# Slot layer of a transformer decoder: the statistics of a later pair's x are issued ahead of the candidate's input on VectorE

## The reference

```python
x = x + slot_layer(_layernorm(x, axis=-1))

def _layernorm(x, axis=-1, eps=1e-05):
    m = jnp.mean(x, axis=axis, keepdims=True)
    v = jnp.var(x, axis=axis, keepdims=True)
    return (x - m) / jnp.sqrt(v + eps)

def slot_layer(x):                         # per sequence, 64 slots
    h = gelu(ctx @ w1.T + b1)              # ctx: x beside the mean of the slots
    route_logits = (h @ w2.T + b2) / (abs(tau) + 0.1)
    topk_vals, topk_idx = top_k(route_logits, 8)
    alpha = softmax(topk_vals) scattered to the 64 slots
    gi = (alpha.T @ x) / (alpha.sum(axis=1) + 1e-08)
    r = sigmoid(xr + hr)                   # a GRU cell: gx = gi @ w_ih.T + b_ih, gh = S @ w_hh.T + b_hh
    z = sigmoid(xz + hz)
    n = tanh(xn + r * hn)                  # the candidate
    h_new = (1.0 - z) * n + z * hs
    return alpha @ (h_new @ wv.T + bv) @ wo.T + bo
```

## Time and profile before

| | us |
|---|---|
| median of 3 runs | 1517.61 |
| the runs | 1512.31, 1517.61, 1517.75 |
| time of the profiled execution | 1513.51 |
| its span, first to last instruction | 1511.8 |
| slot layer's statistics and steps, from the first f_stats to the end | 1218.0 to 1511.8 |
| f_stats of the slot layer, 64 instructions | 0.41 each |

### The profile page before, as it was taken

One profiled execution on the slowest core, in us unless ns is written; L12 is line 12 of the kernel. 1 busy time (PEld: TensorE's weight loads), 2 busy tenths in 40 slices (PEclk: granted clock), 3 DMA queues, 4 the chain that ended last, 5 costly groups with the idle time before them and its releaser, 6 DMA issues. The chain is left out here.

```text
span 1511.8 us, 57218 instructions
## 1 busy us (share of the span) xinstructions
PE 1416.7 (94%) x22238; PEld 1064.8 (70%) x22238; DVE 1101.2 (73%) x3030; ACT 888.3 (59%) x1541; POOL 873.5 (58%) x1184
## 2 busy tenths in 40 slices
PE   6999999999999999985999999999999859999997
PEld 4777777777777777764777777777777636666664
DVE  6777777777777777653667676767676658989896
ACT  3555555555555555542666666666667347777773
POOL 3455555555555555542577777777777635555543
PEclk9999999999999999998999999999999969999998
DMA  5400000000000000003000000000000000010101
GB/s 165 135 2 1 0 0 0 0 0 0 0 0 0 0 0 0 2 3 120 17 24 14 21 14 21 14 21 14 21 14 8 2 1 29 29 35 28 35 28 42
DMA packets 31207, 32.40 MB, mean 21 GB/s; under 512 B 3937, under 2 KB 29602, under 8 KB 31138
## 3 DMA queue, kind: packets, MB, share of 16 engines
q1 hardware_dynamic: 31138, 31.46, 6.9%
HBM read 23.06 MB, written 8.39 MB: 21 GB/s over the span
## 5 line engine op out<-in xcount | busy, mean ns | idle before, releaser
L1028 POOL TENSOR_SCALAR_AFFINE_SELECT a_probs_t<-a_probs_t 128x512 f32<-128x512 f32 x256 | 161.9, 666 | 77.8 <-ACT a_probs_t L697 77.8
L1560 DVE TENSOR_REDUCE c_neg_max<-score_banks 128x8 f32<-128x512 f32 (+1 forms) x128 | 116.3, 950 | 80.2 <-PE score_banks L1292 80.2
L1042 POOL TENSOR_TENSOR a_less<-a_attn,a_remote 128x512 f32<-128x512 f32 x32 | 40.8, 1275 | 218.0 <-DVE a_attn L873 218.0
L1713 POOL TENSOR_SCALAR_AFFINE_SELECT c_probs_t<-c_probs_t 128x512 f32<-128x512 f32 x256 | 154.7, 639 | 12.3 <-ACT c_probs_t L1487 12.1
L1487 ACT ACTIVATE c_probs_t<-score_banks 128x2048 f32<-128x2048 f32 x64 | 120.2, 1879 | 27.2 <-PE score_banks L1320 27.2
L384 PE MATMUL side_banks<-a_xn_t,a_w_qk 128*128 128x256 f32 x512 | 134.4, 398 | 1.7 <-ACT a_xn_t L642 0.7
L697 ACT ACTIVATE a_probs_t<-score_banks 128x2048 f32<-128x2048 f32 x64 | 120.2, 1878 | 25.9 <-PE score_banks L541 25.9
L850 DVE TENSOR_REDUCE a_neg_max<-score_banks 128x8 f32<-128x512 f32 (+1 forms) x128 | 116.4, 951 | 6.0 <-PE score_banks L511 6.0
L384 PEld LDWEIGHTS side_banks<-a_xn_t,a_w_qk 128*128 128x128 f32 x512 | 93.0, 196 | 13.1 <-issue 2.4
L2141 POOL TENSOR_TENSOR r_hn<-rz_t,half_hn 128x256 f32<-128x256 f32 x32 | 23.4, 730 | 123.4 <-ACT rz_t L1970 123.4
L652 ACT ACTIVATE a_k_z<-side_banks,a_b_k,row_half 128x256 f32<-128x256 f32 x128 | 61.8, 562 | 54.0 <-PE side_banks L384 54.0
(11 more groups left out here) (263 smaller groups left out, 3927.7 us busy)
## 6 DMA issues: line engine op xcount, KB each, us to landing
x_sb<-in_x SPq DMA_DIRECT2D x32, 256.0 KB, 2.9
c_ctx_in<-in_ctx SPq DMA_DIRECT2D x32, 256.0 KB, 2.7
out<-y SPq DMA_DIRECT2D x32, 256.0 KB, 2.1
w_ih<-in_ffn_w_ih SPq DMA_DIRECT2D x1, 768.0 KB, 6.4
w_hh<-in_ffn_w_hh SPq DMA_DIRECT2D x1, 768.0 KB, 7.1
a_raw_qk<-in_attn_qk_w SPq DMA_DIRECT2D x1, 512.0 KB, 4.3
a_raw_cross<-in_xattn_qk_w SPq DMA_DIRECT2D x1, 512.0 KB, 4.7
b_ih<-in_ffn_b_ih SPq DMA_DIRECT2D x1, 384.0 KB, 6.1
```

The source lines that it names most:

```text
L1028: nc.gpsimd.affine_select(out=probs, in_=probs, pattern=[[0, 4], [1, 128]], compare_op=ALU.is_ge, fill=0.0, base=-1, channel_multiplier=-1 ...
L1560: ins = nc.vector.tensor_reduce(neg_max[:, tt, :].rearrange("p (i s l) -> p i s l", i=4, s=2)[:, :, :, late], all_scores[:, :, :, 128 * (1 ...
L1713: nc.gpsimd.affine_select(out=heads, in_=heads, pattern=[[0, 4], [1, 128]], compare_op=ALU.is_ge, fill=0.0, base=0, channel_multiplier=-1) ...
```

## The change

In VectorE's `step`, the call of `candidate(updated)` moves from ahead of `norm_stats(second)` to behind it. The wait for the routing logits and the wait for the moments stand ahead of `norm_stats` as before, and so ahead of the candidate now. No instruction is added, removed or resized; the order of the other engines is the same.

```diff
                 if norms:
                     norm_moments()
-                if updated.real:
-                    candidate(updated)
                 if routed.real:
                     dve.wait_ge(logit_ready, routed.count(1, 1))
                 if at.real and second.real:
                     dve.wait_ge(ln_step, following.count(2, 2))
                     norm_stats(second)
+                if updated.real:
+                    candidate(updated)
                 if routed.real:
                     route_top(routed)
                     route_mark(routed)
```

## The result

The changed kernel takes 1521.51 us (median of 8 runs, 1516.55 to 1524.26); the kernel before took 1514.11 us beside it (8 runs, 1512.15 to 1517.75). The ratio is 1.0038 with a 95% interval of 1.0023 to 1.0053: 5.8 us slower, within 0.5%. The two medians lie 7.4 us apart and the means of the runs 5.9 us; the ratio goes with the means. The profiled execution took 1516.55 us.

A forecast was written before the change was run, and what follows sets the result against it. A ring through n_in, h_n, f_x_bias and f_xn was taken as the bound, not VectorE. Terms 0.9 + 1.95 - 0.5 = +2.3 us on 1513.5 gave 1515.8; forecast 1517.8, between that and 1519.9, range 1511.5 to 1524.

The forecast's parts named there:

- The ring: Slot step: chain from rz through n_in, h_n, f_x_bias, both f_xn and back to rz sets its 8.32 us.
- Step one: Ahead of n_in: f_stats waits 0.15 us behind f_moments, so n_in is 0.31 us late in the loop.
- third rival: At n_in: hardly late, 0.08 us in the loop, f_xn stays held; +1 us, 1514.5; 0.13 with mixtures within 0.5%.
- Step two: At f_x_bias: first f_xn slips in ahead, second waits; 0.25 us gained against 0.31 lost, net +0.06 a step.
- first rival: At f_x_bias: f_xn loses its turn in every step; +6.1 us, 1519.6; chance 0.33.
- The sum: Whole layer: inner steps +0.9, first and written-out steps +1.95, step 3 -0.5, total +2.3 us.
- the inner steps' term: Loop: 15 inner steps at +0.06 us each, +0.9 us.
- The two groups of times: Kernel before: its four times fall into 1512.3 and 1513.5, 1517.6 and 1517.8; a median after may lie in either.
- second rival: VectorE's list: it is the bound and the gap is filled; 11 us less, 1502.2; chance 0.09.

The follow-up runs named there:

- late_only: Changed kernel with the pair of f_stats done a second time behind n_in, into a spare tile: 1518.62 us, ratio 1.0047 to the kernel before.
- turn: Changed kernel with slot_val placed between the two f_xn, so the first is issued while h_n works: 1513.51 us, ratio 0.9979 to the kernel before.
- wait_hn: Changed kernel with one more wait on POOL, f_x_bias waiting until h_n is written: 1520.09 us, ratio 1.0052 to the kernel before.
- split: Changed kernel with one f_stats left ahead of n_in and the other put behind it: 1516.79 us, ratio 0.9999 to the kernel before.
- park_split: Changed kernel with one f_stats on each side of n_in and f_x_bias at the head of POOL's step, double-buffered: 1506.26 us, ratio 0.9934.

## Why the prediction was right and where it was wrong

**The bound was right.** The ring over n_in, h_n, f_x_bias and the end of f_xn fits every run in which f_x_bias stands behind h_n: late_only added 0.66 us of VectorE work for nothing, and only the three kernels with f_x_bias parked went clearly below 8.3 us a step. One partner was overlooked: in the kernel before neg_top lasts 0.33 us in place of 0.17, held by h_n, so work taken from behind n_in meets a first stop there and a second at f_x_bias.

**Step one was right.** f_stats starts 0.14 us behind the second f_moments in the loop (taken: 0.15); n_in is 0.30 late in inner steps (0.31), 0.14 in a round's first (0.14), 0.25 in written-out steps (0.25). The chain of waits of the changed kernel shows the register work ahead of f_stats (start, length):

```profile
1308.29 0.06 DVEq L1992
1308.35 0.05 issue
1308.40 0.10 DVE f_stats L1992
```

The Trainium skill's rule that a semaphore between VectorE instructions costs nothing extra ("VectorE: DVE Perf Modes", "The DRAIN you can't avoid") would have put f_stats ahead of f_moments' end, as neighbours without a wait stand. It came 0.14 us behind it in the loop, and 0.10 (rz + 2.58 against 2.48) where there is no register work. The trace disagrees with the rule for this pair, and the third rival falls with it.

**Step two failed**, where it said "I take it that the first f_xn slips in between h_n and f_x_bias". The places were forecast well: slot_val at rz + 4.55 both in forecast and trace, f_xn issued 0.05 us ahead of f_x_bias (forecast 0.06). In the other inner steps the lead was 0.02 or 0.03. But f_xn lost its turn in every inner step, lasting 1.43 to 1.47 us. I took the recorded starts for the order of asking, on the strength of one row of another shape in another layer. The rows of the c_xn pair, which I also leaned on, don't show a thin lead: there the first c_xn starts 0.43 us ahead of POOL's c_summed (767.99 against 768.42), as far as in turn. Leads of 0.02 to 0.07 us lose, leads of 0.17, 0.34 and 0.45 win. The argument that the prediction gave the first rival, that part of an f_xn's 0.40 us passes before it touches what POOL holds, is the one that fits; the f_xn of wait_hn that runs through its first 0.09 us beside h_n unheld bears it out. Why a_gate got through with 0.02 us was not tried. The Trainium skill's rule ("SBUF — State Buffer", "Who interferes with whom") says that whoever issues first holds the lock for a whole instruction. The second half agrees with every row here; the first half holds only if issue isn't read as the start that the profile records.

**The sum.** With the turn lost, each of the inner steps costs nearly n_in's whole delay (0.28 of 0.30 us), not 0.06. Turn gave 0.25 us of it back, by the order on VectorE alone and with n_in as late. The first rival's sum was +6.1 us; measured +5.8, of which +5.6 stand in the slot steps. Its terms measured: 15 inner steps 4.3 (4.65), first steps of rounds 0.6 (0.7), written-out steps 1.1 (1.25; step 28 has a delay of 0.18 and lost 0.15), step 3 -0.56 (-0.5), and +0.2 in the last three steps, where n_in was 0.06 to 0.08 late, which no term had. The forecast's own sum was +2.3, so the inner steps' term, +0.9 where 4.3 was measured, is the one that failed. The time, 1521.5 us, lies in the range on its upper side, and that is no merit of the forecast: the top of the range was taken from the first rival and from the spread of the runs. The two groups of times that stood behind the 1517.8 were an accident of four runs: in the 19 runs taken later the kernel before fills the space between them, from 1512.56 to 1519.16 us.

**The second rival** (VectorE bound, 11 us gained) is refuted for this kernel by the loss itself and by late_only. In the kernel with f_x_bias parked the same edit gains 12.7 us, about what this rival had promised; whether VectorE's list is the bound there was not shown.

## What to carry to other kernels

A gap on a busy engine is worth filling only if no later instruction swallows what is won: compare each instruction's length in the step with its shortest (f_xn 0.72 against 0.40, neg_top 0.33 against 0.17), since a wait for the other engine hides in the length and counts as busy. Find the partner of that wait and move it to where it meets nobody, before reordering the engine that waits: the same reordering cost 5.8 us with f_x_bias in place and gained 12.7 with it moved. And don't let a forecast rest on a lead of a few hundredths of a microsecond: here 0.07 us lost the turn and 0.17 won it.

## What the runs showed of the hardware

- An f_xn issued 0.07 us ahead of POOL's instruction, with nothing of POOL's running, was held for the whole of it (1.49 us, wait_hn); one issued 0.17 ahead was not.
- An instruction on two numbers for each partition is held as well: neg_top takes 0.17 us alone, 0.33 beside h_n in the kernel before and 0.66 in split and park_split.
- POOL is lengthened in turn when a VectorE instruction has just got in ahead of it: f_x_bias took 1.31 us in turn and 1.36 in step 6 of wait_hn, against 1.26.
- A wait of POOL for its own h_n put the start of f_x_bias 0.25 us behind h_n's end in the loop, where without the wait it starts 0.03 ahead of it. In steps written out, which have no register work there, it came 0.14 behind.
- The matmuls of L1886 in the last step took 2.07 us at a granted clock of 0.50 (kernel before) and 1.13 at 1.00 (changed). Where the clock falls differs between executions: at 1499.95 in the one and 1508.82 in the other.
